# Two MLP units built by halves of their rows, a transfer moved behind the restack, one sum moved to GpSimd

## The reference, cut to what matters

```
xn = layernorm(x)                                  # x: 4 x 256 x 256
q, k, v = split(xn @ Wqkv.T)                       # 16 heads of 16
s = softmax(q @ k.T / 4) @ v, heads joined, @ Wproj.T + bproj
h = gelu(xn @ proj1.T + b1)                        # 1024 hidden
g = silu(h @ proj2.T + b2)
out = x + s * g
```

## Time and profile before

| | |
|---|---|
| median of 3 runs | 120.86 us (120.67 to 120.93) |
| the profiled execution | 120.73 us |
| its span, first to last instruction | 118.9 us, 1.8 us less than its time |
| TensorE matmuls busy | 113.7 us (96% of the span) |
| VectorE, ScalarE, GpSimd busy | 84.8, 74.3, 70.3 us |
| TensorE's share of the chain that ended last | 91% |

### The profile page before, as it was taken

One profiled execution on the slowest core, in us unless ns is written; L12 is line 12 of the kernel. 1 busy time (PEld: TensorE's weight loads), 2 busy tenths in 40 slices (PEclk: granted clock), 3 DMA queues, 4 the chain that ended last, 5 costly groups with the idle time before them and its releaser, 6 DMA issues.

```text
span 118.9 us, 2560 instructions
## 1 busy us (share of the span) xinstructions
PE 113.7 (96%) x930; PEld 88.4 (74%) x930; DVE 84.8 (71%) x159; ACT 74.3 (62%) x109; POOL 70.3 (59%) x91
## 2 busy tenths in 40 slices
PE   6989999999999999999999999999999999999980
PEld 5589998887878987888768777776775867566660
DVE  0799994520997989999899498205955848998762
ACT  4063795469979302231295979899868888799000
POOL 4227678009999904877889759589614341517460
PEclk9999999999999999999999999999999999999999
DMA  2999932666565366520000004500000000020213
GB/s 107 298 366 375 330 88 68 205 201 205 203 207 205 121 207 206 199 90 6 7 13 3 0 0 145 215 8 8 11 0 0 0 6 0 13 75 9 85 58 121
DMA packets 9632, 13.27 MB, mean 112 GB/s; under 512 B 2452, under 2 KB 4884, under 8 KB 9492
## 3 DMA queue, kind: packets, MB, share of 16 engines
q1 hardware_dynamic: 9332, 12.85, 32.5%
q10 hardware_dynamic: 288, 0.26, 0.7%
HBM read 5.51 MB, written 1.05 MB: 55 GB/s over the span
## 4 chain that ended last, share of the span: by engine, by line
PE 91%; DVE 2%; DMA 2%; issue 1%; POOL 1%; DVEq 0%; POOLq 0%
PE bank L794 39%; PE bank L903 14%; PE bank L920 12%; PE bank L884 9%; PE bank L870 8%; PE bank L900 6%; DMA xs<-x 2%; PE bank L827 2%; PE bank L931 1%; DVE fin L766 1%; DVE stats L608 1%; POOL rstd L392 1%; DVE fin L775 0%; PE bank L831 0%; DVE xs L623 0%
## 5 line engine op out<-in xcount | busy, mean ns | idle before, releaser
L687 DVE TENSOR_REDUCE negm<-bank 128x4 f32<-128x1024 f32 x32 | 37.3, 1216 | 9.8 <-PE bank L870 9.8
L451 POOL TENSOR_TENSOR hTl<-hG,hTh 128x512 fp32r<-128x512 f32 x16 | 20.4, 1295 | 8.7 <-ACT hTh L564 8.4
L903 PE MATMUL bank<-w2s,hTh 128*128 128x512 f32 x64 | 23.7, 410 | 0.0
L575 ACT ACTIVATE PT<-bank 128x1024 f32<-128x1024 f32 x16 | 15.4, 1027 | 2.8 <-PE bank L884 2.7
L900 PE MATMUL bank<-w2s,hTl 128*128 128x256 f32 x64 | 16.6, 280 | 0.0
L903 PEld LDWEIGHTS bank<-w2s,hTh 128*128 128x128 f32 x64 | 11.7, 188 | 3.1
L560 ACT ACTIVATE hG<-bank,b1s 128x512 f32<-128x512 f32 x16 | 10.9, 683 | 3.5 <-PE bank L794 3.4
L900 PEld LDWEIGHTS bank<-w2s,hTl 128*128 128x128 f32 x64 | 12.1, 188 | 0.5
L884 PEld LDWEIGHTS bank<-qs,ks 50*128 50x128 f32 x128 | 8.4, 185 | 3.8 <-issue 1.4
L884 PE MATMUL bank<-qs,ks 50*128 50x256 f32 x128 | 11.0, 299 | 0.0
L870 PEld LDWEIGHTS bank<-ks,qs 48*128 48x128 f32 x128 | 8.3, 185 | 3.3 <-issue 2.8
(11 more groups left out here) (94 smaller groups left out, 228.7 us busy)
## 6 DMA issues: line engine op xcount, KB each, us to landing
qs<-stage SPq DMA_DIRECT2D x24, 128.0 KB, 2.8
ks<-stage SPq DMA_DIRECT2D x24, 128.0 KB, 2.9
xs<-x SPq DMA_DIRECT2D x4, 256.0 KB, 3.9
w_raw<-w SPq DMA_DIRECT2D x1, 1024.0 KB, 7.5
w_in_place<-w SPq DMA_DIRECT2D x1, 1024.0 KB, 10.0
xb<-x SPq DMA_DIRECT2D x1, 1024.0 KB, 6.3
wqkv_raw<-wqkv SPq DMA_DIRECT2D x3, 256.0 KB, 4.6
out<-fin SPq DMA_DIRECT2D x6, 128.0 KB, 1.7
```

Source lines behind the costliest of these rows:

```text
L451: nc.gpsimd.tensor_tensor(hTl[:, n % FC, :], hG[:, n % FC, :], hTh[:, n % FC, :].bitcast(f32), ALU.subtract).then_inc(h_lo, 1)
L575: nc.scalar.activation(exp_of(w), scores_of(*s), ACT.Exp).then_inc(exp_done, 1)
L687: nc.vector.tensor_reduce(negm[:, j, :, s[1] % 2, b, :], scores_of(*s), axis=AX.X, op=ALU.max, negate=True).then_inc(max_done, 1)
L903: m = nc.tensor.matmul(bank_of("F2", u, 0), hTh[:, fc, c:c + P], w2s[:, fc].rearrange("p a e -> p (a e)"), start=fc == 0, stop=fc == FC - 1)
```

## The change

`F1 2` and `F1 3` become one step at the place of `F1 2`. Each product over 128 rows is cut into two over 64 rows, in the form of the scores. In a first turn the upper 64 rows work for `F1 2` and the lower 64 for `F1 3`, in a second turn the other way round, so that the two halves of the array never write one bank together. Between the turns TensorE waits until both chains of the first are complete. It waits for both banks before the first matmul, and tells ScalarE of both units at the end (`f1_made` goes from 2 to 4).

The two transfers of ones go behind all 48 transfers of the restack. Tile 6 joins `ON_POOL`: its last sum is GpSimd's. The product of tile 7 with the gate stays in PSUM, and the sum reads it there; the wait for the store of tile 3 moves from the product to the sum.

```
-ON_POOL = (2, 3, 4, 5)
+ON_POOL = (2, 3, 4, 5, 6)
@@ sync: the block below stands behind the restack's loop instead of before it
             sp.wait_ge(ones_ready, 1)
             for par in range(2):
                 sp.dma_start(ks[64 * par + STK:64 * par + STM, :, :]..., ones[...]).then_inc(ones_rows, 16)
@@ scalar
-                    act.wait_ge(f1_made, n_f1 + 1)
+                    act.wait_ge(f1_made, 4 if n_f1 == 2 else n_f1 + 1)
@@ vector
-                    if u >= 4:
+                    if 4 <= u < TT - 1:
                         dve.wait_ge(stored[u - 4], 16)
-                    nc.vector.tensor_tensor(fin[:, u % 4, :], spot("PJ", u), gate[:, u, :],
-                                            ALU.mult).then_inc(gated, 1)
+                    nc.vector.tensor_tensor(fin[:, u % 4, :] if u < TT - 1 else spot("PJ", u), spot("PJ", u),
+                                            gate[:, u, :], ALU.mult).then_inc(gated, 1)
...
+                    if u == TT - 1:
+                        dve.wait_ge(stored[u - 4], 16)
+                    nc.vector.tensor_tensor(fin[:, u % 4, :], fin[:, u % 4, :] if u < TT - 1 else spot("PJ", u),
+                                            xb[:, u, :], ALU.add).then_inc(fin_done, 1)
@@ tensor
+                elif s in (("F1", 2), ("F1", 3)):
+                    if s[1] == 3:
+                        continue
+                    both = (s, ("F1", 3))
+                    for one in both:
+                        wait_free(one)
+                    for turn in range(2):
+                        if turn == 1:
+                            pe.wait_ge(f1_half, 2)
+                        for a, b in ((0, 0), (1, 0), (0, 1)):
+                            for kc in range(KC):
+                                for half in range(2):
+                                    one = both[turn ^ half]
+                                    rows = slice(64 * half, 64 * half + 64)
+                                    n = (a, b, kc)
+                                    m = nc.tensor.matmul(bank_of(*one),
+                                                         (w1h, w1l)[a][rows, kc, one[1] * P:(one[1] + 1) * P],
+                                                         (xTh, xTl)[b][rows, kc, 0:HALF],
+                                                         start=turn == 0 and n == (0, 0, 0),
+                                                         stop=turn == 1 and n == (0, 1, KC - 1))
+                                    if n == (0, 1, KC - 1):
+                                        m.then_inc(f1_made if turn == 1 else f1_half, 1)
```

More of the change, by code:

```diff
@@ L211, in layer_kernel @@
         stacked = [[sem(f"stacked{h}{q}") for q in range(2)] for h in range(2)]
-        ones_rows = sem("ones_rows")
+        ones_rows, f1_half = sem("ones_rows"), sem("f1_half")
         s_made, max_done, st_made, exp_done = sem("s_made"), sem("max_done"), sem("st_made"), sem("exp_done")
@@ L342, in _ @@
                     sp.dma_start(wps[row:row + HN], wp[src:src + HN]).then_inc(wp_in, 16)
[L343 to L347, removed]
             for q in range(2):
@@ L360, in _ @@
                                              ).then_inc(stacked[h][q], 16)
+            sp.wait_ge(ones_ready, 1)
+            for par in range(2):
+                sp.dma_start(ks[64 * par + STK:64 * par + STM, :, :].bitcast(f32)
+                             .rearrange("p h (b t) -> p (h b) t", t=SQ),
+                             ones[0:2, None, :].to_broadcast([2, HP * B, SQ])).then_inc(ones_rows, 16)
             for j in range(HP // 2):
@@ L774, in _ @@
                     dve.wait_ge(xb_done, u + 1)
-                    nc.vector.tensor_tensor(fin[:, u % 4, :], fin[:, u % 4, :], xb[:, u, :], ALU.add).then_inc(fin_done, 1)
+                    if u == TT - 1:
+                        dve.wait_ge(stored[u - 4], 16)
+                    nc.vector.tensor_tensor(fin[:, u % 4, :], fin[:, u % 4, :] if u < TT - 1 else spot("PJ", u),
+                                            xb[:, u, :], ALU.add).then_inc(fin_done, 1)
         @block.tensor
```

## The result

The changed kernel takes 122.85 us (median of 4 runs, 122.63 to 123.12), the kernel before beside it 120.77 us (120.39 to 120.93). The ratio is 1.0184, 95% interval 1.0164 to 1.0204: slower, by 2.1 us between the medians. The forecast was 122.6, in a range from 121.8 to 123.2. The profiled execution took 122.63 us.

A forecast was written before the change was run, and what follows sets the result against it. TensorE, 96% busy and back to back after 7 us, was taken to bound the kernel. +1.23 (up to `S 0`) + 0.94 (echo) - 0.12 (restack) - 0.30 (tail) = +1.75 us; forecast 122.6, range 121.8 to 123.2.

The forecast's parts named there:

- (a): Joined units' matmuls: 12 half-row pairs cost the same as the 12 full matmuls, 0.00 us, bounds 0.00 and +0.09.
- (b): Ahead of the joined units' first pair: TensorE waits for the gelu of `F1 1` to free bank 7, +0.97 us.
- (c): Boundary between the two turns: completing the last pair, release and a dearer first pair, +0.35 us, bounds 0.20 and 0.50.
- (d): Turn into half-row shape: 0.09 hidden behind the bank wait, `S 0` saves its 0.20; net -0.09 us.
- (e): At `F1 5`: ScalarE hears of both units late, its queued gelus and roundings echo +0.94 us; delay there 2.17.
- Rival A: Only the bank wait counts, ScalarE keeps up without echo: +0.81 us, 121.7; chance 8%.
- (f): At `F1 6` and later units: the delay grows no further, `F1 6` free by 0.3 us.
- Part 2: Ones moved behind the restack: the wait at `S 18` to `S 20` goes, -0.12 us, bounds 0 and -0.13.
- Part 3: Tail behind the last matmul: VectorE gains 0.36 us, closely issued stores may slow each other; -0.30 taken.
- B: Clock rival: TensorE, after idling, gets half its clock from 27.35 to 31.4 us; about 126 us; chance 5%.
- C: Not-slower rival: the restack sets the pace from `S 0` to `S 20`, its gain covers TensorE's delay; 120.6 us; 4%.
- D: Half-row pairs with full 512 columns don't run together: 2.7 us more, 125.3 us; chance 3%.

The follow-up runs named there:

- The other banks: Changed kernel with `F1 0` and `F1 1` put in banks 2 and 3: 122.06 us, ratio 1.0117 to the kernel before.
- Without the exchange: Changed kernel, each array half writing one bank in both turns, no wait between turns (units get halves of one another's sums): 122.48 us, ratio 1.0163.
- the earlier roundings: Changed kernel with both roundings of `w2s` on ScalarE put ahead of the gelu of `F1 2`: 121.96 us, ratio 1.0106.
- the restack alone: Kernel before with only the ones' transfers moved behind the restack: 120.64 us against 120.58, ratio 1.0001.
- the repairs: Changed kernel with `F1 0`, `F1 1` in banks 2 and 3, and both `w2s` roundings ahead of `F1 2`'s gelu; run singly, and together 121.42 us, ratio 1.0061.

## Why the prediction was right, step by step

- **What bounds it**: right. TensorE had next to nothing to give back, and what it lost at `F1 5` (2.26) is what the last matmul lost (2.32).
- **(a), the pairs**: 0.23 each against 0.227; some 0.05 over all, inside the bounds of 0.00 to 0.09.
- **(b), the wait for both banks**: +1.03 (3.75 - 2.72), forecast 0.97. The missing 0.06 is the release: the gelu ends at 26.85 and the pair starts at 26.99, 0.14 later, where I took 0.08 from a fill by VectorE. The other banks took the wait away and 0.85 of the time with it.
- **(c), the boundary**: from first pair to second turn 1.71, forecast 1.72. Without the exchange 0.32 of the time goes, forecast 0.33 to 0.35.
- **(d), the shape**: 0.09 for the way in without a wait to hide it (2.81 - 2.72), and `S 0` 0.22 behind the last pair, without the extra of a first pair. As reckoned.
- **(e), the echo**: `F1 5` +2.26, forecast +2.17. The difference was there before the echo: 0.06 from the release in (b), the rest from the pairs and the hand-over to ScalarE. At `F1 5` itself 0.14 passed behind the gelu (33.30 to 33.44), as the sum had it for release and restart together; another 0.07 came behind its first matmul. The gelu of `F1 3` ended 2.87 after the start of that of `F1 2` (33.30 - 30.42), forecast 2.88. Rival A is refuted by this, and the earlier roundings show it to be ScalarE's order.
- **(f)**: nothing grew at `F1 6`.
- **Part 2** took 0.12 too much off. The wait at `S 20` did go, but the time came back at `F1 9` to `F1 10`, which wait for ScalarE; and the wait was peculiar to the one trace that I read. I also took 1.48 us as the most the queue could gain, where the last restack transfer landed 3 to 5 us earlier (below); that had no price in the sum. And `S 0` is not always free of the restack, as two traces with the ones ahead show.
- **Part 3, the tail**: the term that was wrong. VectorE's part came as reckoned (0.35, with product and sum in PSUM at 0.43 and 0.42), but I took -0.30 for the end and it is -0.02. The sentence that two stores within 0.1 us "may slow each other" was the mechanism, priced at 0.06 where it costs 0.34. A sum reading PSUM ran freely beside GpSimd (0.42 beside 0.72). The Trainium skill, "SBUF — State Buffer", Who interferes with whom, says the same of a VectorE instruction with a single SBUF input.

By the traces the change costs 2.32 - 0.02 = 2.30, against 1.75 in the sum: 0.28 from the tail, 0.12 from `S 20`, and 0.15 from the release, the pairs and the restart behind `F1 5`. The medians differ by 2.08 only. The 0.2 between is of the size by which executions differ in their start; what it is was not shown. So that the forecast came within 0.25 us (122.6 for 122.85) is partly luck: its three errors all have one sign and sum to 0.55.

Rivals B, C and D fell: the clock stayed full, the restack alone brought 1.0001, the pairs ran side by side. One argument against B was misread. The wait of 0.3 us at 6 us was followed by slow matmuls: the first transposes start 0.2 us apart until 6.8 us and 0.11 apart from then on, and the trace has a record of the granted clock, full, only from 6.8 us, so the digits before that show nothing. TensorE had been at the slow level (1.2 GHz) since its start. The trace of after has the better argument: its first matmuls go from 0.43 to 0.21 us apart at 4.2 us, TensorE then waits 0.9 us for `xs`, and goes on at 0.11 to 0.15.

## What to carry to other kernels

Where two steps are joined into one, list what the first one's run time used to cover (here the second's bank) and when the next engine first hears of a result; both prices came from there (0.85 and 0.73 us by the repairs), and the new form of the matmuls was nearly free. Work that stands between two urgent instructions in an engine's own order belongs into the pause ahead of them. At the end of a kernel an engine's gain counted only where the last two stores did not leave together (0.09 us apart it was lost, 0.5 apart kept): finish one tile early instead of two at once.

## What the runs showed of the hardware that was not expected

The last two stores, 128 KB each from two queues, landed after 1.90 and 2.04 us when issued 0.09 us apart (within 0.03 the same in five more traces); in the kernels that issued them 0.5 to 0.9 us apart, after 1.70 to 1.73. The distance is not all: tile 4's store, the first from ScalarE's queue, took 2.1 to 2.3 in every trace, with the next one mostly 0.7 us behind it; why was not looked into. And two transfers of 64 KB, in pieces of 1 KB onto two rows each, held up much more than their issue time of 1.48 us. The queue with the ones ahead and behind, here in the changed kernel:

```profile
14.33 3.85 SPq L353 DMA_DIRECT2D qs<-stage  x6
...
46.91 1.91 SPq L359 DMA_DIRECT2D ks<-ones  x2
```

The first six issues of the restack take 3.85 us instead of 7.48 (3.85 to 4.81 in the six traces with the ones behind, 7.26 to 7.61 in the seven with them ahead); the last transfer landed at 49.4 us with the ones moved alone, and at 54.6 before (52.1 to 53.4 in other executions with the ones ahead). The busy share of the 16 DMA engines, in tenths of 40 slices, while the six are issued: before (14.7 to 22.3 us), then with the ones moved alone (14.4 to 18.4 us).

```profile
DMA  8553211111111684111111411674212116844855
```

```profile
DMA  9979786654311065973445956545595344594744
```

Before, the share is 35% at 104 GB/s, against 60% at 183 GB/s, and for long stretches it stands at one tenth, which is one or two of the 16 engines. This looks as if a few engines carried the ones' pieces while the queue behind them waited; it was not tested.
